# Halves of four sequences as token tiles in a float32 Flamingo layer: weights turned on VectorE, value products on tiles of 32x64

## The reference

```python
# cross-attention
q, k = rmsnorm(layernorm(x) @ Wq, gq), rmsnorm(ctx @ Wk, gk);  v = ctx @ Wv
x = x + tanh(g_xattn) * (softmax(q @ k.T / sqrt(128)) @ v) @ Wo
# self-attention, causal; y = layernorm(x)
h = rmsnorm(y, ln1_w);  q, k, v = h @ wq, h @ wk, h @ wv
y1 = y + (softmax(where(causal, q @ k.T / sqrt(128), -1e9)) @ v) @ wo
# experts
t = rmsnorm(y1, ln2_w)
x = x + tanh(g_ffn) * (y1 + sum_e cw_e * down_e(silu(gate_e(t)) * up_e(t)) + shared(t))
```

## Time and profile before

| What | Value |
|---|---|
| median of 3 runs (lowest, highest) | 628.91 us (628.39, 629.61) |
| the profiled execution's own time | 628.85 us |
| its span, first to last instruction | 627.1 us |
| busy TensorE | 619.1 us (99%) |
| busy VectorE | 462.0 us (74%) |
| busy ScalarE | 320.5 us (51%) |
| busy GpSimd | 253.3 us (40%) |
| granted TensorE clock over the span | 1.0 |

### The profile page before, as it was taken

One profiled execution on the slowest core, in us unless ns is written; L12 is line 12 of the kernel. 1 busy time (PEld: TensorE's weight loads), 2 busy tenths in 40 slices (PEclk: granted clock), 3 DMA queues, 4 the chain that ended last, 5 costly groups with the idle time before them and its releaser, 6 DMA issues.

```text
span 627.1 us, 18234 instructions
## 1 busy us (share of the span) xinstructions
PE 619.1 (99%) x7200; PEld 541.5 (86%) x7200; DVE 462.0 (74%) x930; ACT 320.5 (51%) x699; POOL 253.3 (40%) x336
## 2 busy tenths in 40 slices
PE   8999999999999999999999999999999999999997
PEld 6788888888889988999999889988888888888886
DVE  5979777997886886786677899565576987555556
ACT  6867677777743334242434333453477444444442
POOL 3221211313144334344343354345545665455453
PEclk9999999999999999999999999999999999999999
DMA  7532131111021322222231321123323233333332
GB/s 234 186 85 70 52 103 28 40 40 31 24 70 43 111 69 69 70 68 77 64 118 39 115 70 36 35 63 93 98 85 94 75 102 101 90 87 99 100 87 90
DMA packets 36023, 50.30 MB, mean 80 GB/s; under 512 B 4080, under 2 KB 23024, under 8 KB 35952
## 3 DMA queue, kind: packets, MB, share of 16 engines
q1 hardware_dynamic: 35376, 48.81, 26.2%
q10 hardware_dynamic: 576, 0.48, 0.2%
HBM read 48.22 MB, written 1.05 MB: 79 GB/s over the span
## 4 chain that ended last, share of the span: by engine, by line
PE 96%; DVE 1%; ACT 1%; DMA 1%; issue 1%; SPq 0%; DVEq 0%; ACTq 0%
PE acc L568 26%; PE bank_q L541 17%; PE bank_k L541 14%; PE bank_v L541 9%; PE bank_s L541 8%; PE bank_v L656 7%; PE bank_k L736 2%; PE bank_p L753 2%; PE bank_s L714 2%; PE bank_s L704 2%; PE bank_t L721 1%; PE bank_p L687 1%; PE bank_q L677 1%; PE bank_k L666 1%; DMA xt<-in_ctx_t 1%
## 5 line engine op out<-in xcount | busy, mean ns | idle before, releaser
L568 PE MATMUL acc<-wo_hi,pv_hi 128*128 128x256 f32 x328 | 93.4, 285 | 0.4 <-DVE pv_lo L1515 0.2
L568 PE MATMUL acc<-wo_lo,pv_hi 128*128 128x256 f32 x328 | 92.9, 283 | 0.0
L568 PE MATMUL acc<-wo_hi,pv_lo 128*128 128x256 f32 x328 | 92.0, 281 | 0.0
L1677 POOL TENSOR_TENSOR wq_lo<-raw_a,wq_hi 128x256 fp32r<-128x256 f32 x32 | 23.4, 732 | 116.9 <-DVE wq_hi L1452 116.9
L568 PEld LDWEIGHTS acc<-wo_hi,pv_hi 128*128 128x128 f32 x328 | 61.5, 188 | 5.3 <-issue 2.2
L1677 POOL TENSOR_TENSOR wq_lo<-raw_m,wq_hi 128x256 fp32r<-128x256 f32 x50 | 40.4, 808 | 59.8 <-DVE wq_hi L1471 58.3
L568 PEld LDWEIGHTS acc<-wo_lo,pv_hi 128*128 128x128 f32 x328 | 61.6, 188 | 2.2
L568 PEld LDWEIGHTS acc<-wo_hi,pv_lo 128*128 128x128 f32 x328 | 62.3, 190 | 0.0
L1515 DVE TENSOR_TENSOR pv_lo<-raw_a,pv_hi 128x512 fp32r<-128x512 f32 (+1 forms) x51 | 37.5, 737 | 31.8 <-ACT pv_hi L1104 31.5
L1104 ACT ACTIVATE pv_hi<-raw_a 128x512 fp32r<-128x512 f32 (+1 forms) x51 | 31.7, 623 | 56.1 <-DVE raw_a L1510 50.5
L541 PE MATMUL bank_q<-xt_hi,wq_hi 128*128 128x512 f32 x144 | 59.8, 415 | 0.0
(11 more groups left out here) (246 smaller groups left out, 1949.2 us busy)
## 6 DMA issues: line engine op xcount, KB each, us to landing
raw_m<-in_chunk_m SPq DMA_DIRECT2D x50, 256.0 KB, 2.8
raw_a<-in_head_a SPq DMA_DIRECT2D x48, 192.0 KB, 3.3
raw_b<-in_head_b SPq DMA_DIRECT2D x32, 256.0 KB, 3.0
raw_m<-in_chunk_m SPq DMA_DIRECT2D x50, 128.0 KB, 2.1
raw_v<-in_pair_v SPq DMA_DIRECT2D x16, 256.0 KB, 2.8
raw_b<-in_head_b SPq DMA_DIRECT2D x32, 128.0 KB, 2.1
xs<-in_x SPq DMA_DIRECT2D x6, 128.0 KB, 3.2
out<-xs SPq DMA_DIRECT2D x3, 256.0 KB, 2.5
```

Of the source, the lines that this page charges most:

```text
L568: last = nc.tensor.matmul(acc[t // 2][:, (t % 2) * D:(t % 2 + 1) * D], w[:, tok], m, start=begins and n == 0, stop=True, skip_group_check= ...
L1677: nc.gpsimd.tensor_tensor(lo, raw, hi, ALU.subtract).then_inc(signal, 1)
```

## The change

The host lays the tokens out in another order: a tile of 128 tokens now holds 32 tokens (one half) of each of four sequences, and the output is put back likewise. In this order a variance lies on the partitions where it is wanted, so `place_variance` goes. The blocks of 32x32 that VectorE turns are now what the self-attention needs as well: `turn_attn` and `take_turned` go, and `turn_weights` serves both attentions. The value products become tiles of 32 keys by 64 columns of the head width, four sequences by two column groups, first the early keys for both halves of queries, then the late keys added for the late queries alone. They need four banks of 256 columns, `bank_k`, `bank_v` (or `bank_q`), `bank_p` and `bank_t`, with the waits that go with that. Rounding and remainder of the results are four instructions of 256 columns each. The output weights are rounded on ScalarE (`round_out`) instead of VectorE. On VectorE `split_head_values` moves ahead of `subtract_max`, and the first `take_q` ahead of `normalise`. On the way to the experts `gate` moves up on ScalarE, and the first up projections take their two banks in the other order.

```diff
+        def tokens_of(ap, j):
+            return ap.rearrange("p h (t j q) -> p h t j q", j=QUADS, q=GROUP)[:, :, :, j, :]
+        def queries_at(n, part, j):
+            at = (n * 2 + part) * P + j * GROUP
+            return slice(at, at + GROUP)
...
         def turn_banks(u):
-            return (bank_t, bank_p) if u.kind == "a" else (bank_p, bank_s if u.kind == "b" else bank_t)
+            return (bank_t, bank_p) if u.kind == "a" else (bank_p, bank_t)
-        def value_bank(h):
-            return (bank_p, bank_t)[h]
+        def head_bank(u, j):
+            return (bank_k, bank_v if u.deferred else bank_q, bank_p, bank_t)[j]
+        def by_token(bank):
+            return bank[:, 0:HT // 2].rearrange("p (h t q) -> p h t q", h=2, q=GROUP)
         def key_bank(u, h):
...
-            return (bank_s, bank_q)[h] if u.very_first else bank_k
+            return (bank_s, bank_q if u.very_first else bank_k)[h]
         def up_bank(u):
-            return (bank_k, bank_s)[u.parity]
+            return (bank_s, bank_k)[u.parity]
# TensorE
             def project_keys(u, h):
-                if h and bank is bank_k and u.kind == "b":
-                    pe.wait_ge(B["kt"], u.of(0))
+                if not h and u.kind == "b" and not u.very_first:
+                    pe.wait_ge(B["scaled"], u.n - 1)
             def norm_q(u):
-                if u.first:
-                    place_variance(u)
             def head_values(u):
                 pe.wait_ge(B["vs"], 2 * u.n)
                 pe.wait_ge(B["attn_t"], u.n)
+                if u.deferred:
+                    pe.wait_ge(B["vs"], 2 * u.n + 2)
+                else:
+                    pe.wait_ge(M["silu"], 1)
-                for g in range(G):
-                    h, n = divmod(g, NT)
-                    for c in range(P // SEQ):
-                        for r in range(SPB):
-                            rows = slice(r * SEQ, (r + 1) * SEQ)
-                            last = nc.tensor.matmul(value_bank(r)[c * SEQ:(c + 1) * SEQ, cols], values[rows, n, width],
-                                                    turned[rows, n, h], start=True, stop=True)
+                for h in range(2):
+                    for n in range(2):
+                        for k in range(2):
+                            for c in range(P // SEQ):
+                                width = slice(h * P + c * SEQ, h * P + (c + 1) * SEQ)
+                                for j in range(QUADS):
+                                    rows = slice(j * GROUP, (j + 1) * GROUP)
+                                    found = by_token(head_bank(u, j))[c * SEQ:(c + 1) * SEQ, h, 2 * n + k:2 * n + 2]
+                                    last = nc.tensor.matmul(found, values[rows, 2 * n + k, width],
+                                                            turned[rows, h, n, k, k:], start=k == 0, stop=True,
+                                                            skip_group_check=True)
             def self_pair(u):
                     project_gate(nxt)
+                    pe.wait_ge(B["scaled"], u.n)
                     project_up(nxt)
-                turn_attn(u)
             def chunk(u):
                 if u.very_first:
+                    pe.wait_ge(B["pv_lo"], QUADS * (prev.n - 1) + 1)
                     project_up(nxt, range(1))
# ScalarE
             def take_head_values(u):
-                for r in range(SPB):
-                    nc.scalar.activation(by_sequence(pv_hi[:], r), by_tile(value_bank(r)[:]), ACT.Copy).then_inc(B["pv_hi"], 1)
+                for j in range(QUADS):
+                    nc.scalar.activation(tokens_of(pv_hi[:], j), by_token(head_bank(u, j)), ACT.Copy).then_inc(B["pv_hi"], 1)
+            def round_out(u, h):
+                if u.n > 1:
+                    act_e.wait_ge(B["wo_done"], u.of(h) - 2)
+                act_e.wait_ge(ld_b2[h], 16 * u.n)
+                nc.scalar.activation(wo_hi[h][:], raw_b2[h][:], ACT.Copy).then_inc(B["wo_hi"], 1)
             def self_pair(u):
+                if nxt.kind == "m":
+                    gate(nxt)
                 prepare(u)
-                take_turned(u)
                 prepare(u, 1)
+                for h in range(2):
+                    round_out(u, h)
...
                 if not u.deferred:
-                    gate(nxt)
                     take_head_values(u)
# VectorE
             def turn_weights(u):
+                stage = stages[u.kind]
                 if u.n > 1:
-                    v.wait_ge(A["pv_done"], u.n - 1)
-                v.wait_ge(A["norm"], u.n)
+                    v.wait_ge(stage["pv_done"], u.n - 1)
+                elif u.kind == "b":
+                    v.wait_ge(A["pv_done"], u.prev().n)
+                v.wait_ge(stage["norm"], u.n)
             def self_pair(u):
                 take_max(u)
-                subtract_max(u)
                 if prev.kind == "b":
                     split_head_values(prev)
+                subtract_max(u)
                 if nxt.kind == "b":
                     split_values(nxt)
+                    take_q(nxt, 0)
                 normalise(u)
-                if nxt.kind == "b":
-                    take_q(nxt, 0)
+                turn_weights(u)
...
-                for h in range(2):
-                    split_out(u, h)
# host
-    x = a["x"].reshape(-1, a["x"].shape[-1])
+    x = a["x"].reshape(-1, 4, 2, SEQ // 2, D).transpose(0, 2, 1, 3, 4).reshape(-1, D)
```

More of the change, by code:

```diff
@@ L337, in flamingo_layer @@
         B = stage_sems("b", "wq_hi wq_lo wk_hi wk_lo wv_hi wv_lo wo_hi wo_lo q_done k_done v_done qt kt vs scores scaled "
-                       "max sub exp sum inv norm t_done attn_t pv_done pv_hi pv_lo wo_done")
+                       "max sub exp sum inv norm attn_t pv_done pv_hi pv_lo wo_done")
         M = stage_sems("m", "wg_hi wg_lo wu_hi wu_lo wd_hi wd_lo g_done u_done silu weighted hh hh_hi hh_lo down")
@@ L581, in output @@
                 else:
-                    pe.wait_ge(B["pv_lo"], u.of(1))
+                    pe.wait_ge(B["pv_lo"], QUADS * u.n)
                     pe.wait_ge(B["wo_lo"], u.of(h))
@@ L711, in scores @@
                     for j in range(QUADS):
-                        at = (2 * j + n) * SEQ
-                        queries = slice(at + part * GROUP, at + (part + 1) * GROUP)
-                        last = nc.tensor.matmul(bank_s[j * GROUP:(j + 1) * GROUP, g * SEQ:g * SEQ + seen], qt[:, h, queries],
-                                                kt[:, h, at:at + seen], start=True, stop=True)
+                        keys = kt[:, h].rearrange("p (n a j c) -> p n j a c", a=2, j=QUADS, c=GROUP)[:, n, j, 0:part + 1]
+                        last = nc.tensor.matmul(bank_s[j * GROUP:(j + 1) * GROUP, g * SEQ:g * SEQ + seen],
+                                                qt[:, h, queries_at(n, part, j)], keys, start=True, stop=True)
                 last.then_inc(B["scores"], 1)
-            def turn_attn(u):
-                pe.wait_ge(B["norm"], u.n)
-                for b in range(G // 2):
-                    last = nc.tensor.transpose(bank_t[:, b * P:(b + 1) * P],
-                                               attn[:, 2 * b:2 * b + 2, :].rearrange("p t k -> p (t k)"), ident)
-                last.then_inc(B["t_done"], 1)
             def context_values(u):
@@ L767, in prepare @@
                 piece, step = piece_at(u)
-                if piece in ("turn", "logits", "spread") and u.kind == "b":
-                    pe.wait_ge(B["scaled"], u.n)
                 if piece == "turn":
@@ L803, in release @@
                     pe.wait_ge(semaphore, value)
-            def place_variance(u):
-                pe.wait_ge(eps_ready, u.half + 1)
-                variance = eps_var[:, u.half, :].rearrange("p (n t) -> p t n", n=2)
-                for j in range(QUADS):
-                    for part in range(2):
-                        row = j % 2 * SEQ + part * GROUP
-                        nc.tensor.matmul(bank_q[j * GROUP:(j + 1) * GROUP, HT // 2 + part * 2:HT // 2 + part * 2 + 2],
-                                         ident[:, row:row + GROUP], variance[:, j // 2], start=True, stop=True)
             def cross_pair(u):
@@ L869, in self_pair @@
                     project_gate(nxt)
+                    pe.wait_ge(B["scaled"], u.n)
                     project_up(nxt)
-                    pe.wait_ge(B["pv_lo"], prev.of(1))
+                    pe.wait_ge(B["pv_lo"], QUADS * prev.n)
                     prepare(u)
@@ L1838 @@
     r = run_bass_kernel_spmd(nc, [{f"in_{n}": laid[n] for n in _INS}], core_ids=[0])
-    return r.results[0]["out"].reshape(inputs["x"].shape)
+    found, shape = r.results[0]["out"], inputs["x"].shape
+    return found.reshape(-1, 2, 4, SEQ // 2, shape[-1]).transpose(0, 2, 1, 3, 4).reshape(shape)
```

55 lines of the change are left out of this document (19 added, 36 removed).

## The result

The changed kernel took 662.14 us (median of 4 runs, 661.13 to 666.0) against 629.26 for the kernel before: a ratio of 1.0536, 95% interval 1.0491 to 1.0581. The forecast was 623.6 us with a range up to 627.6. The change made the kernel slower by 5.4% where I had put 0.85 on faster.

The account below looks back on a forecast made before the run. The prediction took TensorE's issued work as the bound. From 628.85 us: -6.9 turning weights, +1.0 value products, +1.0 one stall, -0.3 variance matmuls gave 623.65, forecast 623.6 us, range 620.9 to 627.6.

Parts of the forecast that it names:

- the value products: Self pairs on TensorE: 128 short matmuls for 64, priced +0.06 us a pair, +1.0 us over 16 pairs.
- Tiles of 32x64: Value products: eight tiles run beside each other, so 128 matmuls again take 16 rounds; part of the +1.0 us.
- Rival C: Value products: eight tiles run by fours, 32 rounds of 58.6 ns, 14.1 us more, 637.7 us; chance 0.07.
- the router: Row used to price value products: 64 matmuls of 16 columns at 8.8 ns each; 128 would take 1.12 us.
- 25 ns a matmul: Value products: 60 cycles of overhead per matmul for the whole array, 3.2 us a pair, some 36 us; not adopted.
- Turning the weights: Self pairs: four TensorE transposes a pair go, one VectorE transpose comes; 0.43 us saved a pair, -6.9 us over 16.
- The new wait ahead of the products: Value products wait for ScalarE's copy out of `bank_v`; 0.17 us of slack, taken as nothing, 3.0 us otherwise.
- Rival A: Value products: the new waits eat half the gain or more, some 626.5 to 628.5 us; chance 0.10.
- Return of the values: Self pairs: the last split of values ends 0.59 us before the output that needs it; taken as nothing.
- Rival B: Self pairs: VectorE's later softmax or the values' return is late, pairs stay at 13.78 us, about 629.5; chance 0.05.
- Output weights on ScalarE: Casts delay the second value projection in the second half's first self pair: one stall, +1.0 us (bounds 0 and 1.5).

Follow-up runs that it names:

- aligned kernel: Changed kernel plus idle identity products in seven self pairs, so that no instruction block should end between a pair's scores and value products: 644.16 us, 1.0227.
- shifted: Changed kernel with the scores of the very first cross pair issued twice, 128 more instructions or half a block: 656.61 us, 1.0431.

## Why the prediction was wrong

*What failed: the value products, +1.0 us with bounds of -3.0 and +2.9.* I priced 128 matmuls by their rounds and left out that their instructions have to be brought to TensorE, in blocks. The term measured some +36.5 us in the profiled execution, in three parts. Stops among the products of pairs 1 to 14 come to 20.7 us by the distances between starts, 20.6 beyond the steps that pair 4 has at the same places. Six stretches of half clock cost 1.5 to 1.6 us each, 9.4 together (pair 9: 18.08 - 13.72 - 2.79 of stop = 1.57). And the products run slower: first to last start is 1.35 us in undisturbed pairs, where I had 1.00 and an upper bound of 1.12, 16 x 0.41 = 6.5 us over the 0.94 of the earlier trace rows. The experiments show that the stops come from the number and place of instructions. That the half clock follows from the stops is read from its place in each trace where it occurs, among them those of the aligned kernel and of the one with late keys left out; it is not shown, and stops of up to 2.5 us went by without it. Why the products run slower is open.

There was a row for it, in the waits of TensorE in the kernel before:

```profile
PE bank_t L753 <- issue: 0.2, 1, 0.2
```

It lies among the value products of pair 4 and is of the same kind: a block's transfer began 2.2 us earlier. I gave a stall that small no price. It should have been scaled by the products' instructions, which the change doubled from 128 to 256 with their loads: before, with a burst of 256 instructions (scores and products), one pair stopped; with one of 384, twelve did.

The Trainium skill, "Runtime: NRT & Kernel Launch", section "Instruction fetch mechanics", says that instructions are brought in blocks of 16 KiB, 256 at a time, by an own DMA queue while the block ahead is executed, and that crossing a boundary is mostly hidden. Block and count agree with the 24 and 31 instructions above. The cost doesn't: up to 3.0 us were not hidden here, and the measurement decides. I didn't weigh that section of the Trainium skill.

*Tiles of 32x64.* Right: eight run beside each other. In pair 1 the first eight start within 0.06 us of 202.43 and the ninth at 202.54; the first 32 matmuls of an undisturbed pair start within 0.24 us. Rival C, which had the slower side, is refuted in its mechanism, and its 637.7 would still have been too low. What failed is the rest: the next 96 take 1.11 us, 11.5 ns each and not the 8.8 of the router. What holds them is not settled. The prediction set aside 25 ns a matmul, some 36 us in all; that this is near the measured term is chance, since the starts are 7.8 to 11.5 ns apart in an undisturbed pair and 30 of the 36.5 us are stops and half clock.

*Turning the weights, -6.9 us.* Right, and hidden by the line above: an undisturbed pair went from 13.78 to 13.72 (13.72 to 13.82 in the shifted and aligned kernels) with +0.41 in the products, so the other parts saved 0.37 to 0.47 where I had 0.43. The slower products alone took this back: 0.4 us is what the prediction named as the point from which the change loses. With the products as before, a pair takes 13.32 to 13.42 us.

*The new wait ahead of the products, nothing.* Right: they begin 0.88 us after the scores in both kernels, and no wait for `vs` stands there. Rival A did not occur as told: it had TensorE without the products' instructions for a signal that came late, and here TensorE lacked them with no signal late.

*Return of the values, nothing.* Right: no wait for it is added in the self pairs. Rival B did not occur; VectorE is less busy than in the earlier trace rows.

*Output weights on ScalarE, one stall of +1.0 us in the ninth pair.* Right in place and nearly in size. In pair 8, on both engines:

```profile
321.08 0.72 ACT L1070 ACTIVATE wo_hi<-raw_b 128x256 fp32r<-128x256 f32 x2
321.35 0.39 PE L547 MATMUL bank_k<-xt_hi,wk_lo 128*128 128x512 f32 x1
321.71 0.58 ACT L1029 ACTIVATE vs<-bank_v 128x512 f32<-128x512 f32 x1
322.43 0.36 PE L662 MATMUL bank_v<-wv_hi,xt_hi 128*128 128x256 f32 x1 [0.69 <-ACT vs L1029]
```

The copy of the values stands behind the two casts. 322.43 - 321.35 is 1.08 us, the usual step there is 0.23: 0.84 us lost. The casts' part is shown, 0.61 us; the 0.2 that I gave to VectorE's transposes is near the 0.23 left, which no run separates.

*The whole.* From the first scores of the self pairs to those of the last, the stage is 30.9 us longer (239.55 for 208.69): 20.6 of stops, 9.4 of half clock, 0.8 for ScalarE and 0.9 for a stop in a projection of pair 6, less 0.06 in each pair and the 0.4 that pair 4 lost before, make some 30. Another 2.0 us lie behind it, 1.3 of them the last pair's stop.

## What to carry to other kernels

Count the instructions of a burst, weight loads too, beside its busy time. In the self pairs of these kernels TensorE came from one block boundary to the next, 256 instructions, within 2.2 us 28 times, and stopped at the second for over 0.3 us in 27; at 2.2 to 4.7 us it stopped at some. A matmul of 64 rows cut into two of 32 doubles the count. A wait called "issue" that is short and happens once is a limit that is near; scale it with the instructions before pricing it at nothing. And lay a long stop's price higher than its length: here six of the eight stops of 1.7 us and more had half clock behind them, for another 1.6 us each.

## What the runs showed of the hardware that was not expected

- TensorE went on 2.2 to 3.3 us (mostly 2.3 to 2.5) after the start of a block's transfer in the stops of eleven kernels, though such a transfer is recorded with 0.9 to 1.9 us. What decides when a transfer starts is open: after a boundary it mostly took 0.4 to 2.4 us, in stretches of long projections up to 8.
- 1,096 additional instructions made a kernel 18 us faster, by the place of its block boundaries alone.
- A VectorE transpose of 32 partitions took 433 ns for 256 columns and 304 for 128 (mean), where 128 partitions by 512 columns took 711: eight small ones are 3.0 us.
